# Slot sums of a soft mixture of experts: kept by ScalarE and added by GpSimd instead of VectorE

## What is computed

```python
logits = (einsum('tzd,ed->tze', x, phi_w) + phi_b).reshape(t, z, n, p)
D = softmax(logits, axis=3)          # dispatch, over the slots of an expert
C = softmax(logits, axis=2)          # combine, over the experts of a slot
X_tilde = einsum('tznp,tzd->npd', D, x)      # 2048 slot sums over all tokens
X_tilde = tanh(normalise(clip(X_tilde)))
Y_tilde = einsum('npd,ndH->npH', X_tilde, expert_w) + expert_b[:, None, :]
Y = einsum('tznp,npH->tzH', C, Y_tilde)
```

## Time and profile before

| | |
|---|---|
| median of three runs | 1049.57 us (1048.29 to 1051.22) |
| profiled execution, its own time | 1050.74 us |
| its span | 1049.0 us |
| busy: TensorE, VectorE, ScalarE, GpSimd | 953.9, 752.7, 483.3, 459.6 us |
| share of the span | 91%, 72%, 46%, 44% |
| mean granted TensorE clock | 0.958 of 2.4 GHz |

### The profile page before, as it was taken

One profiled execution on the slowest core, in us unless ns is written; L12 is line 12 of the kernel. 1 busy time (PEld: TensorE's weight loads), 2 busy tenths in 40 slices (PEclk: granted clock), 3 DMA queues, 4 the chain that ended last, 5 costly groups with the idle time before them and its releaser, 6 DMA issues.

```text
span 1049.0 us, 22748 instructions
## 1 busy us (share of the span) xinstructions
PE 953.9 (91%) x8338; PEld 809.2 (77%) x8338; DVE 752.7 (72%) x1095; ACT 483.3 (46%) x768; POOL 459.6 (44%) x375
## 2 busy tenths in 40 slices
PE   7389999999997558799999999999998997999997
PEld 6278888887885346688887888888887756999997
DVE  1746767667663398899998999999998553544442
ACT  1145555555553144565565565566556233333331
POOL 0422222222220077687786787777777341010100
PEclk9689999999998788999999999999999998999999
DMA  9201111111110402223323223323325894776660
GB/s 303 73 21 36 42 42 42 40 41 40 41 33 29 103 10 56 58 79 92 80 61 88 68 67 90 82 60 86 91 62 180 318 410 145 236 224 240 220 201 23
DMA packets 97688, 110.42 MB, mean 105 GB/s; under 512 B 12148, under 2 KB 88980, under 8 KB 91684
## 3 DMA queue, kind: packets, MB, share of 16 engines
q1 hardware_dynamic: 95460, 102.31, 31.7%
q10 hardware_dynamic: 800, 3.74, 1.0%
q0 software_dynamic: 1376, 3.70, 0.9%
HBM read 71.51 MB, written 38.21 MB: 105 GB/s over the span
## 4 chain that ended last, share of the span: by engine, by line
DVE 26%; PE 24%; issue 11%; POOL 3%; ACT 2%; DVEq 0%; DMA 0%; POOLq 0%; ACTq 0%
PE slots_p_turn L1200 15%; DVE slots_dmax L811 6%; DVE slots_csum L800 6%; DVE slots_dsum L845 5%; PE slots_p_sum L1092 3%; DVE slots_disp L816 3%; PE slots_logits L1118 3%; DVE xacc L794 3%; ACT slots_comb L1004 1%; PE slots_logits L1167 1%; POOL slots_comb L929 1%; POOL slots_disp L933 1%; DVE slots_xn L784 1%; DVE slots_xt_lo L828 1%; DVE slots_cmax L839 1%
## 5 line engine op out<-in xcount | busy, mean ns | idle before, releaser
L1092 PE MATMUL slots_p_sum<-slots_x,slots_disp 128*128 128x256 f32 (+1 forms) x928 | 208.1, 382 | 6.1 <-POOL slots_disp L933 6.1
L1092 PEld LDWEIGHTS slots_p_sum<-slots_x,slots_disp 128*128 128x128 f32 (+1 forms) x928 | 174.6, 191 | 31.3 <-POOL slots_disp L933 4.7
L937 POOL TENSOR_TENSOR slots_comb<-slots_comb,slots_csum 128x2048 f32<-128x2048 f32 (+1 forms) x29 | 105.0, 3619 | 66.0 <-DVE slots_csum L802 66.0
L929 POOL TENSOR_TENSOR slots_comb<-slots_comb,slots_cmax 128x1024 f32<-128x1024 f32 (+1 forms) x58 | 112.0, 1949 | 44.1 <-DVE slots_cmax L839 44.1
L933 POOL TENSOR_TENSOR slots_disp<-slots_disp,slots_dsum 128x2048 f32<-128x2048 f32 (+1 forms) x29 | 105.8, 3647 | 0.0
L1004 ACT ACTIVATE slots_comb<-slots_logits 128x512 f32<-128x512 f32 (+1 forms) x116 | 66.1, 598 | 85.3 <-DVE slots_disp L816 85.3
L816 DVE TENSOR_TENSOR slots_disp<-slots_logits,slots_dmax 128x512 f32<-128x512 f32 (+1 forms) x116 | 80.2, 691 | 5.9 <-issue 1.9
L964 POOL DMA_DIRECT2D out<-slots_o x29 | 15.9, 548 | 156.3 <-DVE slots_o L899 156.3
L395 POOL TENSOR_TENSOR attend_stack<-attend_rope_a,attend_rope_b 113x256 f32<-113x256 f32 x64 | 45.3, 729 | 88.9 <-DVE attend_rope_b L350 88.9
L978 ACT ACTIVATE slots_ct<-slots_p_turn 128x512 f32<-128x512 f32 (+1 forms) x116 | 64.1, 580 | 38.7 <-PE slots_p_turn L1083 38.6
L811 DVE TENSOR_REDUCE slots_dmax<-slots_logits 128x16 f32<-128x512 f32 (+1 forms) x116 | 78.8, 679 | 3.3 <-PE slots_logits L1118 1.8
(11 more groups left out here) (132 smaller groups left out, 1973.6 us busy)
## 6 DMA issues: line engine op xcount, KB each, us to landing
combine_t<-slots_ct SPq DMA_DIRECT2D x224, 128.0 KB, 2.4
slots_comb<-combine_t SPq DMA_DIRECT2D x14, 1024.0 KB, 5.6
slots_ct<-combine_t SPq DMA_DIRECT2D x14, 1024.0 KB, 5.8
expert_w<-wexp SPq DMA_DIRECT2D x8, 1024.0 KB, 9.1
slots_disp<-wexp SPq DMA_DIRECT2D x8, 1024.0 KB, 13.4
h<-attend_h_out SPq DMA_DIRECT2D x32, 113.0 KB
slots_h_t<-h SPq DMA_DIRECT2D x28, 128.0 KB, 2.2
slots_x<-h SPq DMA_DIRECT2D x28, 128.0 KB, 2.0
```

The costliest lines, as they stand in the source:

```text
L929: nc.gpsimd.tensor_tensor(m, m, cmax[0:rows, shalf(i)].unsqueeze(2).broadcast_to([rows, SLOTS // 2, EXPERTS]), ALU.subtract).then_inc(csub ...
L937: nc.gpsimd.tensor_tensor(m, m, csum[0:rows, 1].unsqueeze(2).broadcast_to([rows, SLOTS, EXPERTS]), ALU.mult).then_inc(comb_ok, 1)
L1092: last = nc.tensor.matmul(p_sum[u % 2][:, i, :], disp[d][0:rows].rearrange("p n s -> p (n s)")[:, 128 * e:128 * e + 128], x[d][0:rows], st ...
```

## The change

The two units that a step sums leave PSUM by ScalarE. `keep_sum` moves from VectorE's stream into ScalarE's. In steps 1 to 4 it copies straight to xacc. From step 5 on it copies to a new SBUF buffer (part_sum, two of them, one for each PSUM buffer), and GpSimd adds that to xacc (`add_sum`). ScalarE's first keep stands behind the second copy of the logits from step 5 on, and behind the fourth in steps 1 to 4; the second keep stands behind the first two quarters. GpSimd's first add stands ahead of its subtraction of the maximum, its second between L933 and L937. The last group stays on VectorE, with a semaphore of its own (last_ok). add_ok counts GpSimd's adds and starts at eight by a one-element memset, so that ScalarE can wait for the part buffer with one rule.

```diff
--- before.py
+++ after.py
@@ -601,6 +601,7 @@
         ct = [sb(f"ct{i}", [128, EB, 128]) for i in range(2)]
         e_stats, e_mv, e_rstd = sb("e_stats", [128, EB, 6]), sb("e_mv", [128, EB, 2]), sb("e_rstd", [128, EB])
         e_power = sb("e_power", [128, EB])
+        part_sum = [sb(f"part_sum{i}", [128, 2, C]) for i in range(2)]
 
         logits = pb("logits", [128, EXPERTS, SLOTS])
         p_turn = [pb(f"p_turn{i}", [128, 4, 128]) for i in range(2)]
@@ -631,6 +632,7 @@
         drec_ok, crec_ok, disp_ok, comb_ok = sem("drec_ok"), sem("crec_ok"), sem("disp_ok"), sem("comb_ok")
         kept_ok, copied_ok = sem("kept_ok"), sem("copied_ok")
         ct_ps_ok, ct_ok, sum_ok, acc_ok = sem("ct_ps_ok"), sem("ct_ok"), sem("sum_ok"), sem("acc_ok")
+        add_ok, last_ok = sem("add_ok"), sem("last_ok")
         eb_in, w_in = sem("eb_in"), [sem(f"w_in{i}") for i in range(WRING)]
         clip_ok, e_stats_ok, e_mv_ok, e_var_ok, e_rstd_ok = sem("clip_ok"), sem("e_stats_ok"), sem("e_mv_ok"), sem("e_var_ok"), sem("e_rstd_ok")
         norm_ok, tanh_ok, t_ps_ok, t_ok = sem("norm_ok"), sem("tanh_ok"), sem("t_ps_ok"), sem("t_ok")
@@ -784,15 +786,6 @@
                 nc.vector.tensor_scalar(xn[par][0:rows], h_t[par][0:rows], mv[0:rows, 0:1], rstd[0:rows],
                                         ALU.subtract, ALU.mult).then_inc(x_ok, 1)
 
-            def keep_sum(s, u):
-
-                part = xacc[:, 2 * u:2 * u + 2, :]
-                dve.wait_ge(sum_ok, val(s + 1))
-                if static(s) and s < UNITS:
-                    nc.vector.tensor_copy(part, p_sum[u % 2][:]).then_inc(acc_ok, 1)
-                else:
-                    nc.vector.tensor_tensor(part, p_sum[u % 2][:], part, ALU.add).then_inc(acc_ok, 1)
-
             def combine_sum(n, par, rows):
 
                 dve.wait_ge(cexp_ok, val(2 * (n + 1)))
@@ -845,8 +838,6 @@
                     nc.vector.reduce_sum(dsum[0:rows, 0], disp[c % RING][0:rows], AX_X).then_inc(dsum_ok, 1)
                     dve.wait_ge(dsum_ok, val(t + 1))
                     nc.vector.reciprocal(dsum[0:rows, 1], dsum[0:rows, 0]).then_inc(drec_ok, 1)
-                for s, u in sums(t, c):
-                    keep_sum(s, u)
 
             steps(dve, step)
             combine_sum(LAST, LAST, 128)
@@ -855,8 +846,10 @@
 
                 blocks = range(2 * u, 2 * u + 2)
                 part = xacc[:, 2 * u:2 * u + 2, :]
-                keep_sum(FINAL + u, u)
-                dve.wait_ge(acc_ok, FINAL + u + 1)
+                dve.wait_ge(sum_ok, FINAL + u + 1)
+                dve.wait_ge(add_ok, FINAL - UNITS + u + 1)
+                nc.vector.tensor_tensor(part, p_sum[u % 2][:], part, ALU.add).then_inc(last_ok, 1)
+                dve.wait_ge(last_ok, u + 1)
                 nc.vector.tensor_scalar(part, part, CLIP_LO, CLIP_HI, ALU.max, ALU.min).then_inc(clip_ok, 1)
                 dve.wait_ge(clip_ok, u + 1)
                 for i in blocks:
@@ -913,15 +906,27 @@
         def _(pool):
             pool.wait_ge(consts, 1)
 
+            nc.gpsimd.memset(part_sum[0][:, 0, 0:1], 0.0).then_inc(add_ok, UNITS)
+
+            def add_sum(s, u):
+
+                pool.wait_ge(acc_ok, val(s + 1))
+                pool.wait_ge(add_ok, val(s - UNITS + 1))
+                part = xacc[:, 2 * u:2 * u + 2, :]
+                nc.gpsimd.tensor_tensor(part, part, part_sum[u % 2][:], ALU.add).then_inc(add_ok, 1)
+
             def step(t, half, c):
                 live, nxt, ahead = flags(t)
                 rows = rows_of(t)
+                units = sums(t, c) if not static(t) or t > TG else []
                 if ahead:
                     arows = rows_of(t + 2)
                     pool.wait_ge(mv_ok, val(t + 3))
                     nc.gpsimd.tensor_tensor(mv[0:arows, 1:2], mv[0:arows, 1:2], eps[0:arows], ALU.add).then_inc(var_ok, 1)
                     pool.wait_ge(var_ok, val(t + 3))
                     nc.gpsimd.tensor_tensor(rstd[0:arows], mv[0:arows, 1:2], power[0:arows], ALU.pow).then_inc(rstd_ok, 1)
+                if units:
+                    add_sum(*units[0])
                 if live:
                     pool.wait_ge(cmax_ok, val(t + 1))
                     for i in range(2):
@@ -932,6 +937,8 @@
                     d = disp[c % RING][0:rows]
                     nc.gpsimd.tensor_tensor(d, d, dsum[0:rows, 1].unsqueeze(2).broadcast_to([rows, EXPERTS, SLOTS]),
                                             ALU.mult).then_inc(disp_ok, 1)
+                    if units:
+                        add_sum(*units[1])
                     pool.wait_ge(crec_ok, val(t + 1))
                     m = comb[c % 2][0:rows]
                     nc.gpsimd.tensor_tensor(m, m, csum[0:rows, 1].unsqueeze(2).broadcast_to([rows, SLOTS, EXPERTS]),
@@ -978,10 +985,21 @@
                 nc.scalar.activation(ct[par][:, 4 * q:4 * q + 4, 0:rows_of(t)], p_turn[q % 2][:, :, 0:rows_of(t)],
                                      ACT.Copy).then_inc(ct_ok, 1)
 
+            def keep_sum(s, u):
+
+
+                act.wait_ge(sum_ok, val(s + 1))
+                to = xacc[:, 2 * u:2 * u + 2, :]
+                if not static(s) or s >= UNITS:
+                    act.wait_ge(add_ok, val(s - 1))
+                    to = part_sum[u % 2][:]
+                nc.scalar.activation(to, p_sum[u % 2][:], ACT.Copy).then_inc(acc_ok, 1)
+
             def step(t, half, c):
                 live, nxt, ahead = flags(t)
                 rows, nrows = rows_of(t), rows_of(t + 1)
                 weights = not static(t) or t >= 1
+                units = sums(t, c)
 
                 def exp_half(buf, cut, before, per, done, i):
                     act.wait_ge(before, val(2 * per * t + per * (i + 1)))
@@ -1003,11 +1021,14 @@
                         act.wait_ge(dsub_ok, val(NB * t + b + 1))
                         nc.scalar.activation(comb[c % 2][0:rows, :, bank(b)],
                                              logits[0:rows, bank(b), :].rearrange("p n s -> p s n"), ACT.Copy).then_inc(copied_ok, 1)
+                        if units and b == (NB - 1 if static(t) and t <= TG else 1):
+                            keep_sum(*units[0])
                     exp_half(disp[c % RING], nhalf, dsub_ok, 2, dexp_ok, 0)
                     exp_half(disp[c % RING], nhalf, dsub_ok, 2, dexp_ok, 1)
                 if weights:
                     keep_quarter(t - 1, (c + 1) % 2, half(-1), 0)
                     keep_quarter(t - 1, (c + 1) % 2, half(-1), 1)
+                    keep_sum(*units[1])
                 for i in range(2):
                     if live:
                         exp_half(comb[c % 2], shalf, csub_ok, 1, cexp_ok, i)
@@ -1146,7 +1167,10 @@
 
                 pe.wait_ge(disp_ok, TILES)
                 pe.wait_ge(kept_ok, TILES)
-                wait_for(pe, acc_ok, FINAL + u - 1)
+                if u < 2:
+                    pe.wait_ge(acc_ok, FINAL + u - 1)
+                else:
+                    pe.wait_ge(last_ok, u - 1)
                 add_products(u, last_group, True, True).then_inc(sum_ok, 1)
 
             def turn(i):
```

## The result

The changed kernel takes 1065.95 us (median of four, 1064.47 to 1066.75), the kernel before 1049.03 beside it: ratio 1.0156, interval 1.0136 to 1.0176. It is 1.6% slower. The profiled execution took 1066.40 us with a span of 1064.7; before it was 1050.74 and 1049.0.

What follows compares the result with a forecast made beforehand. TensorE was taken to bound the loop at 15.41 us a step, VectorE close behind. The terms +14.9 + 1.5 - 3.0 + 1.35 = +14.7 gave 1064.3 us against the median 1049.57, range 1055 to 1076.

Steps and rivals of the forecast that it cites:

- part 1: Steps 5 to 28: VectorE loses its two sum operations, winning back 3.0 us of TensorE's waits, between 0 and 4.1.
- Rival (c): In the loop VectorE, not TensorE, sets the pace; steps fall to 14.12 us, total 1033.5 us; chance 0.07.
- Part 2: Steps 1 to 4: ScalarE's first keep waits for the product with disp's exponentials queued behind it, costing 14.9 us.
- The term from product to L828: Steps 1 to 4: time from the slot product to the next step's low half xt_lo, taken as 10.6 us.
- Cold products in step 5: TensorE idles about 2.9 us before step 5's products, which then run at a lower clock: +1.5 us, between 0 and 1.5.
- Part 3: Steps 5 to 28: ScalarE's keeps do not bound the loop, but cost 1.35 us once in step 28, between 0 and 1.4.
- The tie of 5.34 us: From step 5: VectorE's maximum of comb starts 5.34 us after TensorE's products start, behind the keep and two logits copies.
- Part 4: GpSimd's adds take 1.27 us each, giving a 14.3 us step under 15.41; cost zero, a bound above 1.8 us an add.
- Rival (a): GpSimd becomes the loop's bound, with adds of 2.24 us and a step of 16.3 us: about 1088 us; chance 0.07.
- Rival (b): TensorE's low clock reaches further in steps 1 to 4 as its gaps grow: 12 us more, 1076 us; chance 0.06.
- Rival (d): No change: a small loss in steps 1 to 4 is paid by 3 us in the loop, 1047 to 1052 us; chance 0.06.

Runs made afterwards that it cites:

- the wait alone: The kernel before, with ScalarE in steps 1 to 4 waiting for the first slot sum ahead of disp's exponentials and copying nothing: 1067.07 us, ratio 1.0168.
- the order alone: The changed kernel, with ScalarE's first keep of steps 1 to 4 behind the exponentials of disp instead of ahead: 1048.99 us, ratio 0.9994.
- the runs that have spare adds: Changed kernel with copies of steps 1 to 4 back on VectorE, plus extra GpSimd adds: two a step 1080.29 us, one 1047.06 us.
- Untying ScalarE alone: Changed kernel with copies of steps 1 to 4 back on VectorE, plus first keep behind disp's exponentials from step 5: 1048.44 us, ratio 0.9998.

## Why the prediction was right

1064.3 us were forecast and 1065.95 measured: +14.7 forecast and +16.4 measured against the median shown before (1049.57), +16.9 against that beside the changed kernel. The path was right, and the largest term was 0.9 us too small. That the sum came so close is luck in part. Step 5 was taken 1.1 us too small and the last products 1.35; against them stand 1.2 us too little for part 1 and the 1 us that came back behind the stage. The 1060 to 1069 given for the terms' ends is a slip too: from 1049.57 the ends come to 1060.4 and 1067.4.

- *TensorE is the bound of the loop, at 15.41 us a step.* Held: 15.40 with VectorE idle in each step. Rival (c), that TensorE only follows VectorE, falls by the same row, as TensorE's step did not shrink.
- *Part 1, 3.0 us won back, between 0 and 4.1.* It was 4.2. I left half of the wait at the loop's restart standing, and all of it went. Before, VectorE twice waits there without a releaser (1.51 and 1.87 us, in the rows of before shown above); in the changed kernel no such wait shows at the restart, and TensorE never stops. Why they went is open; in the kernel with the wait alone, whose VectorE stream is that of before, one of 1.71 us is still there.
- *Part 2, 14.9 us in steps 1 to 4.* It was 15.8, and the wait alone and the order alone show the cause. The term from product to L828, 10.6 us, measured 10.5. Undersized was the time until the product: 10.32 us in step 2 and 10.59 in step 1, where I took those of before, 9.86 and 10.06. Step 2 took 17.74 us before, not the 17.39 of step 3 that I put for it, but it grew by the same 3.06.
- *Cold products in step 5, 1.5 us, between 0 and 1.5.* It was 2.6, outside these ends. The row I measured it by had a clock of 0.72 in its first 5 us; here it was 0.50. The length of the wait does not give the size: with the wait alone it was 3.87 us and the 32 products took 9.00, here 3.38 us and 9.89.
- *Part 3.* The tie of 5.34 us measured 5.26 (819.90 - 814.64), the loss in step 28 1.3 for 1.35. Left out were the last products: behind the longer wait there (5.71 us for 4.44) they took 1.35 us more. The last section shows that the same wait has also gone without this loss.
- *Part 4, an add of 1.27 us beside a free GpSimd.* 1.274 us, and no cost. The bound I gave, 1.8 us an add, is near what follows from the runs that have spare adds: (15.40 - 14.2) / 2 + 1.27 = 1.9. Rival (a) falls, as the adds did not stretch in the loop. The Trainium skill, GPSIMD Engine Reference, section Specifications, has GpSimd and VectorE in contention where VectorE has two SBUF inputs or a two-port mode. The trace agrees as far as it goes: 48 adds, beside reductions and instructions that read PSUM, took 1274 ns on average; no run here has one beside a VectorE instruction with both inputs in SBUF.
- *Rival (b), the low clock reaching further.* In part: the products of steps 1 to 4 start 0.1 to 0.5 us later behind L821 than before, 1.3 us in all, with the granted clock over the matmuls of logits at 0.72 to 0.76 where it was 0.75 to 0.80. That is about a ninth of its 12 us. Rival (d) falls: the exponentials and not the copies were what counted, as the wait alone costs as much with the copies left on VectorE.

## What to carry to other kernels

An engine's stream is a queue: moving a PSUM eviction to an idle engine moves its wait too, and what stands behind it pays, here 5 us of exponentials and sum for a copy of 0.6. Look step by step for where the producer comes late (here the four steps with another order), place the eviction behind everything that does not need it, and then look at the next engine's queue, which inherits the wait. Work taken from an engine that is not the bound wins only the stalls that it caused, here 4.2 us for 31 us of VectorE's work.

## What the runs showed that I had not expected

- A longer wait of TensorE can cost twice, but need not. Behind the 5.71 us in front of the last products the granted clock was 0.50 over 5.2 us, and the 48 products took 13.38 us; behind 4.44 us it was 0.72 and 12.03. In the kernels above, waits of up to 4.44 us there gave 12.03 to 12.31 us, waits of 5.48 us and more gave 12.24 to 13.45: three profiles with the same wait of 5.71 us had 13.38, 13.45 and 12.43. With one profile of each version this is a tendency at most, and no price.
- Of VectorE's waits of 1.51 and 1.87 us at the loop's restart, none is left in the versions in which its stream in the loop is without the two sum operations. Six of them have one of 0.49 us in the first step behind the loop. The cause is open.
- Untying ScalarE alone was worth nothing (1048.44 us against 1046.91): the wait had gone over into GpSimd's queue.
